# A three-hop graph layer on one core: five chunks of ten groups in place of four of thirteen, and three softmax stages a step in hops 1 and 2

## The reference

```python
h = relu(layernorm(x))                    # 50000 x 128, the entity table
agg = h; out = 0
for hop in range(3):
    t   = agg[tail]
    att = sum((agg[head] @ q_w) * tanh(rel * t @ k_w), axis=1)
    w   = exp(att - segment_max(att, head)[head])
    w   = w / segment_sum(w, head)[head]          # softmax over the edges of one head
    s   = segment_sum(w[:, None] * rel * t, head)
    agg = s / max(count(head), 1)
    agg = agg / max(norm(agg), 1e-12)
    out = out + agg + h
return x + out
```

## Time and profile before

| stretch, us from the span's start | what | us |
|---|---|---|
| 0 to 222 | sort, indices, first fetches | 222 |
| 222 to 1026 | loop of hop 0, first to last product | 804 |
| 1026 to 1262 | tail of hop 0 | 236 |
| 1262 to 1450 | 12 dense chunks | 188 |
| 1450 to 1779 | loop of hop 1 | 329 |
| 1779 to 1890 | tail of hop 1 | 111 |
| 1904 to 2286 | loop of hop 2 | 382 |
| 2286 to 2566 | tail of hop 2 | 280 |

### The profile page before, as it was taken

How to read it: one execution, slowest core, us unless ns; L and a number is a source line. 1 busy time by engine, 2 the same in 40 slices (tenths; PEclk the granted TensorE clock), 3 DMA queues, 4 the chain that set the end, 5 groups by cost and what they waited for, 6 DMA issues and landing times. The chain is left out here.

```text
span 2566.3 us, 24723 instructions
## 1 busy us (share of the span) xinstructions
PE 1126.9 (44%) x5196; PEld 897.6 (35%) x5196; DVE 1454.0 (57%) x7228; ACT 858.7 (33%) x2657; POOL 1190.2 (46%) x1219
## 2 busy tenths in 40 slices
PE   0112333355454545553100257688734667655430
PEld 0011222244344324453100135467623455454320
DVE  8863664453364545544339657667654644657664
ACT  3312442332333423333126433344433232222320
POOL 1034434454545354466650255552035554647666
PEclk9999655555565655556555577788567777765555
DMA  5532322221222222322225464453144644636654
GB/s 203 207 139 88 129 93 67 68 80 57 71 67 68 71 71 70 115 80 92 77 81 213 172 189 146 132 150 109 63 153 139 189 127 115 174 85 168 168 142 130
DMA packets 192463, 305.35 MB, mean 119 GB/s; under 512 B 31210, under 2 KB 113458, under 8 KB 183686
## 3 DMA queue, kind: packets, MB, share of 16 engines
q1 hardware_dynamic: 153914, 230.79, 26.9%
q0 software_dynamic: 38400, 72.99, 10.8%
HBM read 176.41 MB, written 132.67 MB: 120 GB/s over the span
## 5 line engine op out<-in xcount | busy, mean ns | idle before, releaser
L646 POOL DMA_INDIRECT tr<-in_x_dram,tidx x200 | 191.4, 957 | 508.4 <-DMA acc_d<-xr 297.1
L1574 PE MATMUL ps<-rt,wr 128*125 128x128 f32 x1200 | 266.3, 392 | 245.1 <-issue 85.0
L1503 PE MATMUL ps<-ident,rt 128*128 128x128 f32 x600 | 144.6, 385 | 449.2 <-DVE rt L1169 206.8
L646 POOL DMA_INDIRECT tr<-agg_d,tidx x200 | 191.9, 959 | 288.4 <-DMA agg_d<-rt 138.4
L1574 PEld LDWEIGHTS ps<-rt,wr 128*125 128x125 f32 x1200 | 233.0, 288 | 263.4 <-DVE wr L1094 145.5
L1381 ACT ACTIVATE sqj<-ps,invc 125x128 bf16<-125x128 f32 x600 | 212.3, 373 | 328.5 <-remote 161.1
L646 POOL DMA_INDIRECT tr<-ntab_d,tidx x200 | 193.7, 969 | 260.9 <-DVE rt L1169 196.3
L1341 ACT COPY turns<-ps 128x512 f32<-128x512 f32 x150 | 87.8, 585 | 617.1 <-PE ps L1503 351.1
L1503 PEld LDWEIGHTS ps<-ident,rt 128*128 128x128 f32 x600 | 98.0, 196 | 482.0 <-issue 248.4
L1094 DVE TENSOR_SCALAR wr<-segbc,lcol,wcol 128x125 f32<-128x125 uint8 x600 | 177.9, 349 | 153.7 <-remote 111.4
L658 POOL DMA_INDIRECT ntab_d<-rt,lidx x200 | 202.1, 1011 | 134.2 <-DVE rt L1118 75.1
(11 more groups left out here) (239 smaller groups left out, 2456.2 us busy)
## 6 DMA issues: line engine op xcount, KB each, us to landing
agg_d<-rt SPq DMA_DIRECT2D x100, 258.0 KB
xr<-agg_d SPq DMA_DIRECT2D x100, 258.0 KB
relr<-rel_d SPq DMA_DIRECT2D x100, 256.0 KB
ntab_d<-rt SPq DMA_DIRECT2D x10, 2519.5 KB
acc_d<-xr SPq DMA_DIRECT2D x50, 258.0 KB
rel_d<-relr SPq DMA_DIRECT2D x50, 256.0 KB
hr<-acc_d SPq DMA_DIRECT2D x50, 256.0 KB
hr<-agg_d SPq DMA_DIRECT2D x50, 256.0 KB
```

Source lines behind the costliest of these rows:

```text
L646: G.indirect_dma_start(out=row, out_offset=None, in_=table[:, :], in_offset=bass.IndirectOffsetOnAxis(ap=idx[:, n:n + 1], axis=0)).then_in ...
L1503: ins = T.transpose(ps[B_TR][:, t, :], rt[:, g * GT + t, 0:D], ident[:, :])
L1574: ins = T.matmul(ps[B_T + j % 2][0:R, t, :], wr[:, (j % 2) * GT + t, 0:R], rt[:, j * GT + t, 0:D], start=True, stop=True)
```

## The change

- `K` = 5 chunks of ten groups, 40 tiles each, the last one included. The units of hop 0 are then all of two groups, 25 in place of 27.
- `PLACES` = [3, 3, 3]: hops 1 and 2 get a third place at the end of a step, on PE behind place 1, on DVE behind the step's scaling; ACT's `exps` moves from the place behind `turned` to the end of the step.
- `PARTS` = [40, 20, 20]: a chunk's parts take one step in hop 0, two in hops 1 and 2 (before: two and four).
- `NDE` = 7 early dense chunks for 5, `LATE_AT` = [1, 7, 13]: three late ones in each of hops 1 and 2 for four. `NDB` stays 12.
- `FILL` = [5, 3, 5]: in hop 1 three sums stand behind stages of the last chunk for five.
- The negated masks `gfn` and `gbn` of all chunks give way to `gneg`, made for one chunk in stage 0.

From the tables of the code: the groups summed inside the loops go from 14, 28 and 14 to 15, 34 and 17; the steps that hold a sum in the loops of hops 1 and 2 begin at 18 for 24.

```diff
@@ -23,8 +23,8 @@
 HG = NG // 2
-K = 4
-GC = [0, 13, 26, 39, NG]
+K = 5
+GC = [0, 10, 20, 30, 40, NG]
 TC = [GT * g for g in GC]
@@ -35,7 +35,7 @@
 DE = 16
-NDE = 5
+NDE = 7
 XE = 3
@@ -50,7 +50,7 @@
-LATE_AT = [1, 7, 13, 19]
+LATE_AT = [1, 7, 13]
 NDB = ND - (HOPS - 1) * len(LATE_AT)
@@ -72,10 +72,10 @@
 STAGES = 8
-PLACES = [3, 2, 2]
+PLACES = [3, 3, 3]
 READY_AT = [[[g in u for u in UNITS].index(True) + 2 for g in (GC[c + 1] - 1 for c in range(LAST))],
             [GC[c + 1] + 2 for c in range(LAST)], [GC[c + 1] + 2 for c in range(LAST)]]
-PARTS = [26, 13, 13]
+PARTS = [40, 20, 20]
 EVERY = [1, 1, 2]
@@ -124,7 +124,7 @@
-FILL, HOLD = 5, 2
+FILL, HOLD = [5, 3, 5], 2
@@ -132,7 +132,7 @@
 def sums_mixed(h):
-    return sums_left(h)[FILL:len(sums_left(h)) - HOLD]
+    return sums_left(h)[FILL[h]:len(sums_left(h)) - HOLD]
@@ -141,7 +141,7 @@
-    return sums_left(h)[i:i + 1] if i < FILL else range(0)
+    return sums_left(h)[i:i + 1] if i < FILL[h] else range(0)
@@ -211,10 +211,9 @@
         onesr = sb("onesr", [1, P])
-        gf = sb("gf", [Q, K, R], BF16)
-        gb = sb("gb", [Q, K, R], BF16)
-        gfn = sb("gfn", [Q, K, R], BF16)
-        gbn = sb("gbn", [Q, K, R], BF16)
+        gfb = sb("gfb", [Q, 2, K, R], BF16)
+        gf, gb = gfb[:, 0, :, :], gfb[:, 1, :, :]
+        gneg = sb("gneg", [Q, 2, R], BF16)
         gcol = sb("gcol", [Q, 2, K])
@@ -282,8 +281,8 @@
         LS, LL, LF, LB, LSP = range(5)
-        lx = [chunks_of(28 + 2 * k, P) for k in range(5)]
-        seg0, seg0f, seg0n = (chunks_of(38 + 2 * k, R) for k in range(3))
+        lx = [chunks_of(29 + 3 * k, P) for k in range(5)]
+        seg0, seg0f, seg0n = (chunks_of(83 + 3 * k, R) for k in range(3))
         erow = flat[0:1, 8 * SC:8 * SC + 5 * NT].rearrange("p (k n) -> p k n", k=5)
@@ -917,8 +916,6 @@
             ch(V.memset(gb[:, :, R - 1:R], 0.0))
-            ch.note(V.tensor_scalar(gfn[:, :, :], gf[:, :, :], BIG, -BIG, ALU.mult, ALU.add))
-            ch(V.tensor_scalar(gbn[:, :, :], gb[:, :, :], BIG, -BIG, ALU.mult, ALU.add))
             to_pe()
@@ -945,10 +942,10 @@
                 n, part = CT[b], slice(TC[b], TC[b + 1])
-                marks = (gf, gb) if add else (gfn, gbn)
+                marks = (gf[0:n, b, :], gb[0:n, b, :]) if add else (gneg[0:n, 0, :], gneg[0:n, 1, :])
                 lines = (G_, GN, WGF, WGB) if add else (GNEG, GNNEG, WGFN, WGBN)
                 return (n, (ALU.mult, ALU.add) if add else (ALU.add, ALU.max), 0.0 if add else LOWEST,
-                        [m[0:n, b, :] for m in marks], [rows[:, k, part] for k in lines])
+                        marks, [rows[:, k, part] for k in lines])
@@ -1015,6 +1012,7 @@
                     ask()
+                    ch.note(V.tensor_scalar(gneg[0:n, :, :], gfb[0:n, :, b, :], BIG, -BIG, ALU.mult, ALU.add))
                 elif stage == 1:
@@ -1277,6 +1275,8 @@
                             scaled(h, j)
+                    if h > 0:
+                        softmax(h, *stage_at(h, s, 2))
                     if h == 0 and s in COUNTS_AT:
@@ -1410,14 +1410,14 @@
                             turned(h, s)
-                        if stage_at(h, s, 0)[1] == 3:
-                            exps(h, stage_at(h, s, 0)[0])
                         if 1 <= s <= NG:
...
                             dense(c, range(DC // 2, DC))
+                        if stage_at(h, s, 2)[1] == 3:
+                            exps(h, stage_at(h, s, 2)[0])
                     for j in sums_at(h, s - 1):
@@ -1601,6 +1601,7 @@
                         softmax(*stage_at(h, s, 1))
+                        softmax(*stage_at(h, s, 2))
                     parts(h, *parts_at(h, s))
```

## The result

The changed kernel takes 2669.8 us, the median of four runs (2648.4 to 2684.8), against 2569.4 us of the kernel before in the same comparison. The ratio is 1.039, with a 95% interval of 1.031 to 1.047. The prediction was 2549 us and its range ended at 2600. The profiled execution of the changed kernel took 2648.4 us, the fastest of its four, so the traces show 80 of the 100 us.

The account below looks back on a forecast made before the run. The prediction took the kernel to be bound by chains passing from engine to engine, none busy over 57%. Its terms, +3 - 6 + 5 - 14 + 13 - 20 = -19 against 2568.1 us, gave 2549 us, range 2508 to 2600.

Parts of the forecast that it names:

- hop 0, loop: Loop of hop 0: +3 us, from more groups at the early pace (+7) and a slightly faster late part (-4).
- hop 0, tail: Tail of hop 0: -6 us, as fifteen groups are summed in the loop for fourteen, one scale less.
- hop 1, loop: Loop of hop 1: +5 us, from third places +4, carries +4, a late dense chunk less -3; sums free.
- hop 1, tail: Tail of hop 1: -14 us, from fewer sums among stages, forty tiles of parts, and twelve last groups for thirteen.
- hop 2, loop: Loop of hop 2: +13 us, from six more steps with sums +8, third places +4, carries +4, dense chunk -3.
- hop 2, tail: Tail of hop 2: -20 us, from 39 groups to scale for 42, at 6.7 us each.
- lockstep rival: Hop 0's loop: with pairs only, every unit stays at 36.3 us; +72 in place of +3, 2618 us; chance 0.12.
- steps rival: Hop 0's loop: steps are the cost, two fewer give -46 in place of +3, 2500 us; chance 0.12.
- POOL's wait for L1126: Tail of hop 2: POOL's wait for DVE ahead of its scatters was to fall under 55.6 us.
- The third place: Loops of hops 1 and 2: a third stage a step waits 0.5 us each, +4 us in each loop.
- The loops have no room: Rival: sums and stages moved from tails into loops are paid there in full; +19, 2587 us; chance 0.20.
- The rule: Hop 0's loop: if PE and ACT never wait at memory ports, POOL's bursts cost others nothing; 0 for +3.

Follow-up runs that it names:

- e3: Changed kernel with both settings undone in hops 1 and 2: two stages and ten tile sums a step, five chunks kept; 2576.4 us, ratio 1.007.
- e2: Changed kernel with two stages a step in hops 1 and 2 instead of three, twenty tile sums a step kept; 2619.7 us, ratio 1.028.
- e13: Changed kernel with every second tile sum left out in the loops of hops 1 and 2; 1978.3 us for 1967.6, ratio 1.003.
- e1: Changed kernel with ten tile sums a step in four steps instead of twenty in two, three stages kept; 2612.1 us for 2581.1, ratio 1.025.
- e4: Kernel before with three stages a step in hops 1 and 2, placed as in the changed kernel; 2600.3 us, ratio 1.018.
- e10: The kernel of e3 run again: five chunks, two stages and ten tile sums a step; ratio 1.003.
- before's second trace: The kernel before, unchanged, run again for its own trace; ratio 0.999, loops of hops 1 and 2 at 344 and 384 us.
- e5: The changed kernel, unchanged, run again in another session; 2030.3 us for 1965.6, ratio 1.032.
- e7: Changed kernel with a step's twenty tile sums split on TensorE, ten at its end, ten behind the next step's turn; ratio 1.032.
- e16: The kernel of e7 run again; ratio 1.028.

## Why the prediction was wrong

By its own stretches, each measured to the last product or the last weights, in the two profiled executions:

```
                  forecast   measured
hop 0, loop          +3        +2
hop 0, tail          -6        +1
hop 1, loop          +5       +62
hop 1, tail         -14       -23
hop 2, loop         +13       +59
hop 2, tail         -20       -21
rest                  0         0
sum                 -19       +80
```

**Hop 0 was right**, its loop to 1 us. Four of POOL's twenty bursts are of 32 fetches, the first of them the tenth, and neither the lockstep rival (+72) nor the steps rival (-46) came. The tail's scale wasn't gained in this trace (232.6 for 231.8 us).

**The tails of hops 1 and 2 were right in sign**, hop 2's in size too. Hop 1's terms came near their prices (forty tiles in 17.23 us where 40 x 0.41 = 16.4 stood in the sum). Some 10 us beyond them lie ahead of the first stage, which no term covered: it starts 11 us behind the last product (1844.0, 1854.96), where it started 21 behind before (1778.0, 1799.37). One sign was wrong: POOL's wait for L1126 (L1128 before) is 58.4 us and did not fall under 55.6.

**The loop of hop 1 is the step that failed, +62 for +5**, by two of its terms.

- "PE's parts are 160 tiles in the loop for 156 and count for nothing." I counted tiles and not how many a step holds. Thirteen tiles stood in each of four steps, twenty stand now in each of two. With two stages a step the longer rows cost 83 us over both loops (e3 to e2: 332 + 381 to 372 + 424), some 13 of them at most for the three group sums that come along; half of the tiles left out of the packed steps took 62 us off both loops (e13).
- The third place at 0.5 us a stage, +4. With ten tiles a step it costs 49 us over the loops of both hops (e3 to e1), 6 us a chunk, and 26 to 45 us in the kernel before (e4), 4 to 7.5 a chunk. I priced the wait inside the stage from a scan's 3.32 us and left out what the chain of stages had carried with it: a chunk's six middle stages take 106/4 = 26.5 us as two steps of three (after) and 98/4 = 24.5 as three steps of two (e10), summed from the products' starts. Their length hardly depends on the steps they stand in; with three a step, one ordinary group fewer rides along.

Both are one mistake: I asked what each moved instruction costs and not what a step has room for. The earlier trace rows showed that steps with a sum are as fast as steps without one, and I let that stand for stages and parts too. The rows that would have told are the chunks' own windows: three chunks of before took 180 of hop 1's 328 us in 26 of its 49 steps. At 60 us a chunk, four in six steps each are 240, and 25 others at 6.4 are 160: 400 us, against the 390 measured. That it comes so near is in part luck: those 180 us miss a step of the third chunk, and before's second trace has 66 and 79 us for its two whole chunks.

**The loop of hop 2, +59 for +13**, has the same two terms, and 20 us of it is the 48th product. The last chunk's row of tile sums there falls into POOL's scatters. How many of these stand in one row, and the longest step beside them in us: 20 and 29.4 in before, 24 and 18.2 in e3 (with one of 16.6 ahead of it), 28 and 34.8 in e2, 32 and 40.5 in e1, 36 and 49.7 in after. The order isn't strict: before's second trace has 20 and 24.8. In each of them the product that ends the step comes 5 to 11 us behind the row's last scatter. More groups finished earlier, as the change wants, make the row of scatters longer. That the row holds PE up is read from the traces and was not tried by itself.

**The rivals.** "The loops have no room" had the right side, 2587 us and a chance of 0.20, but not the mechanism: it was to decide where a step with a sum takes over 7.3 us, and steps outside the chunks take 6.1. Its price for moved work was the tail's, while the moved work was a small part of the loss (nine group sums, 38 us of the loops' 121 at that price, and e3 keeps four of the nine with its loops at before's length); the packing of all chunks was the larger, the three old ones too. I should have had "what a chunk's steps hold" as a rival of its own.

**The rule.** The prediction set the Trainium skill's page SBUF — State Buffer, "Who interferes with whom", by which PE and ACT never wait on anyone at the memory's ports, against the pauses behind POOL's bursts. In hop 2's window PE was busy for 3.22 of 37 us beside POOL's scatters, with work in its queue. So something does hold PE back there, by the trace; that it is a port is not shown, and the next section speaks against it.

## What to carry to other kernels

Where engines pass work round in a hand-made pipeline, price a moved operation by what the step that takes it still has room for: sum the steps in which the side work runs, apart from the others, and look whether a step's queue is late or early at its end (does the next instruction wait, as the turn behind ten tiles does, or start at once, as behind twenty). Side work has much of its length to itself, here 60 us a chunk in six steps and 66 in nine; packing it tighter mostly takes away the ordinary steps that it covers. And count the chunks that were there already: a setting that applies to all of them costs on all of them.

## What the hardware showed that I had not expected

**Two speeds of the same kernel.** The changed kernel's median is 2669.8 us in one set of runs and 2030.3 in another, with equal instructions and nearly equal busy times. The page of e5, the changed kernel on the faster kind:

```profile
span 2041.4 us, 25018 instructions
PE 1131.1 (55%) x5256; PEld 904.1 (44%) x5256; DVE 1468.1 (72%) x7366; ACT 860.3 (42%) x2663; POOL 1234.9 (60%) x1219
```

DVE is busy for 1468 us here and 1476 there, so nearly all of the 605 us between the spans is idle time for it; 261 us of them lie in hop 0's loop (803 and 542). At the point of hop 2 where PE crept, POOL scatters here too. The window of e5:

```profile
1759.00:1796.00 37.00, 31.57 (x170) 27.28 (x169) 19.13 (x91) 8.48 (x26) 28.78 (x28) 0.69 0.37 109
```

31.6 us of PE's work beside 28 scatters, where the slower kind did 3.2 beside 26. The same instructions meet here without harm, so the memory's ports alone don't explain it. What differs is not shown, not even whether it is the chip (chip numbers 0 and 5 of the record had both speeds).

**What a row of tile sums costs hangs on the granted clock.** Windows of e5 on two rows, and then on the stretches ahead of each:

```profile
1118.40:1126.90 8.50, 8.50 (x42) 8.50 (x42) 3.29 (x21) 2.15 (x6) 4.84 (x5) 0.50 0.41 110
1183.50:1188.10 4.60, 4.60 (x42) 4.60 (x42) 3.33 (x21) 1.36 (x7) 3.45 (x4) 1.00 0.90 242
1107.00:1118.40 11.40, 5.24 (x21) 3.77 (x21) 6.92 (x39) 2.12 (x6) 4.04 (x5) 0.62 0.38 117
1172.00:1183.50 11.50, 7.26 (x37) 6.24 (x35) 10.70 (x56) 4.17 (x16) 8.86 (x9) 0.59 0.42 108
```

Twenty tiles take 8.5 us at a granted clock of 0.50 (1.2 GHz) and 4.6 at 1.00 (2.4 GHz). Ahead of the slow row PE was busy for 5.24 of 11.4 us, ahead of the fast one for 7.26 of 11.5. Most rows of ten in e10's hop 1 took 2.3 to 2.4 us, the price at full clock; the rows of twenty in after took 4.6 to 6.7. The Trainium skill's page TensorE: Matmul & The Clock Gate, "What's actually happening", says that the slow state is the default and activity releases it; these two rows agree, and two are no test. The rows of hop 1's four chunks sum to 45 us in after and 39 in e10, two of whose rows stand behind the last product, so slower rows are some 6 of the 61 us between these two loops.

The clock counts for more than these rows. Two traces of one kernel, e7 and then e16, in hop 1's loop:

```profile
1010.00:1349.00 339.00, 249.58 (x1293) 201.22 (x1294) 228.01 (x1353) 132.35 (x422) 178.74 (x180) 0.75 0.51 151
1004.00:1321.00 317.00, 225.30 (x1280) 180.45 (x1281) 228.81 (x1353) 130.53 (x415) 182.34 (x183) 0.80 0.56 163
```

PE's busy time differs by 24 us and the loop by 22, with DVE's work the same and a granted clock of 0.75 and 0.80. Of after's 31 us more on PE than e10 in this loop (262.6 and 231.2, clocks 0.72 and 0.78), three group sums are 9 and the 40 records that e10 has behind its last product 5; the rest, some 17 us, is the same work at a lower clock. So part of what the packing costs may come by way of the clock. No run separates it from the rest.
